# Adjacency of a graph layer in one-chunk steps, with one-hots shared by POOL and VectorE and filler products on TensorE

## The reference

```
h = layernorm(x);  q, k, v = linear(h) each
scores = sum(q[dst] * k[src]) / 16 + edge_weight * we + be
attn = exp(scores - segment_max[dst]) / segment_sum(exp)
out = segment_sum(v[src] * attn, dst)
x1 = layernorm(h + out + h @ ws + bs)
x2 = layernorm(x1 + ffn(x1));   x = x + x2
x = x + relu(W2[e] @ relu(W1[e] @ layernorm(x)))    with e = argmax of the router
```

## Time and profile before

| | us |
|---|---|
| median of 3 runs | 1888.78 |
| lowest, highest | 1887.14, 1910.01 |
| span of the profiled execution | 1885.6 |
| TensorE busy in it | 1656.9 |
| VectorE busy | 1193.9 |
| ScalarE busy | 965.5 |
| POOL busy | 300.8 |

### The profile page before, as it was taken

One profiled execution on the slowest core, in us unless ns is written; L12 is line 12 of the kernel. 1 busy time (PEld: TensorE's weight loads), 2 busy tenths in 40 slices (PEclk: granted clock), 3 DMA queues, 4 the chain that ended last, 5 costly groups with the idle time before them and its releaser, 6 DMA issues.

```text
span 1885.6 us, 41069 instructions
## 1 busy us (share of the span) xinstructions
PE 1656.9 (88%) x11015; PEld 1378.6 (73%) x11015; DVE 1193.9 (63%) x3327; ACT 965.5 (51%) x2962; POOL 300.8 (16%) x397
## 2 busy tenths in 40 slices
PE   2898999999799999999899999999999789419960
PEld 1796888888688888887688888888888779315640
DVE  3927898988688889898555555555555578701111
ACT  1566888888588888887233333333333345103210
POOL 0022000000000000000111111111110067375435
PEclk9999999999899999999999999999999889656555
DMA  6054333333433333334822222222210100047634
GB/s 159 28 129 115 104 105 104 106 103 105 140 104 104 106 105 103 104 105 112 164 76 77 76 76 76 76 78 75 76 75 37 53 17 0 6 117 214 181 113 121
DMA packets 226999, 180.40 MB, mean 96 GB/s; under 512 B 41884, under 2 KB 218038, under 8 KB 223544
## 3 DMA queue, kind: packets, MB, share of 16 engines
q1 hardware_dynamic: 189327, 112.46, 21.6%
q0 software_dynamic: 21408, 61.20, 9.7%
q10 hardware_dynamic: 16224, 6.27, 1.5%
HBM read 84.94 MB, written 99.11 MB: 98 GB/s over the span
## 4 chain that ended last, share of the span: by engine, by line
PE 78%; DVE 6%; DMA 5%; POOL 4%; issue 3%; SPq 2%; ACT 1%; POOLq 0%; DVEq 0%; ACTq 0%
PE bank L1371 29%; PE bank L1404 15%; PE bank L1392 11%; PE bank L1356 9%; PE bank L1411 3%; PE bank L1486 3%; PE bank L1493 2%; PE bank L1478 2%; PE bank L1444 2%; PE bank L1436 2%; POOL arena L691 2%; POOL xs_dram L669 2%; SPq L458 1%; DMA V<-in_x 1%; DMA arena<-in_x 1%
## 5 line engine op out<-in xcount | busy, mean ns | idle before, releaser
L784 ACT ACTIVATE arena<-bank,tables 128x128 f32<-128x128 f32 x2048 | 585.2, 369 | 144.5 <-PE bank L1356 144.4
L1371 PE MATMUL bank<-arena 128*125 128x128 f32 x4096 | 585.9, 286 | 11.8 <-DVE arena L1055 11.8
L1371 PEld LDWEIGHTS bank<-arena 128*125 128x125 f32 x4096 | 488.4, 188 | 65.1 <-DVE arena L1055 11.9
L1055 DVE TENSOR_TENSOR arena<-iota_row,tables 128x250 f32<-128x250 f32 x1024 | 421.1, 412 | 0.1
L1081 DVE SCALAR_TENSOR_TENSOR arena<-arena,tables,bank 125x128 f32<-125x128 f32 x1023 | 351.9, 344 | 86.5 <-PE bank L1371 37.1
L1404 PE MATMUL bank<-V,arena 125*125 125x256 f32 x1250 | 296.4, 382 | 5.6 <-ACT arena L810 5.6
L810 ACT COPY arena<-bank 125x500 f32<-125x500 f32 (+1 forms) x175 | 90.8, 533 | 379.5 <-PE bank L1411 379.5
L1404 PEld LDWEIGHTS bank<-V,arena 125*125 125x125 f32 x1250 | 223.3, 188 | 38.0 <-ACT arena L810 10.3
L1122 DVE CUSTOM_DVE_ANT_0 arena<-arena 125x3200 f32<-125x3200 f32 x25 | 87.3, 3493 | 222.2 <-ACT arena L793 222.2
L622 POOL COPY gidx<-arow 125x1 uint32 (+1 forms) x25 | 36.4, 1455 | 1182.2 <-DVE wk_sb L1122 856.7
L1356 PE MATMUL bank<-dist_rhs,arena 5*128 5x128 bf16 x2048 | 201.6, 218 | 4.2 <-DVE tables L1039 3.4
(11 more groups left out here) (219 smaller groups left out, 1665.5 us busy)
## 6 DMA issues: line engine op xcount, KB each, us to landing
adj<-arena SPq DMA_DIRECT2D x512, 125.0 KB
xs_dram<-zeros SPq DMA_DIRECT2D x64, 112.0 KB, 3.2
V<-xs_dram SPq DMA_DIRECT2D x56, 128.0 KB, 2.3
ys_dram<-arena SPq DMA_DIRECT2D x56, 128.0 KB, 1.9
w_dram<-in_L_ffn_W SPq DMA_DIRECT2D x2, 2048.0 KB
V<-in_x SPq DMA_DIRECT2D x5, 625.0 KB
q_dram<-arena ACTq DMA_DIRECT2D x25, 125.0 KB, 2.3
wq_sb<-q_dram SPq DMA_DIRECT2D x25, 125.0 KB, 7.8
```

The lines of the kernel that those rows point to most:

```text
L784: ins = nc.scalar.activation(Ys[:, q, k, :], bank[2 + s][:, k * LO:(k + 1) * LO], ACT.Relu, scale=nval_tab[:, bass.ds(i, 1)])
L1055: ins = V_.tensor_tensor(Xs[:, s, cols, :], iota_row[:, 0:TILE].unsqueeze(1).to_broadcast([P, SUB, TILE]), code_tab[:, bass.ds(g * GC + k ...
L1371: ins = mm(o, Xs[:, j % STAGES, k, :], Ys[:, j % STAGES, k, :], start=(k % SUB == 0), stop=(k % SUB == SUB - 1))
```

## The change

A step has one chunk. The blocks of sources are 128 wide and lie side by side (`HI` = 25 blocks of `LO` = 128), so keys and scores have 25 x 125 = 3125 columns, padded to 3136 = 7 x 448, in place of 25 x 128. There are 1406 steps, 704 groups, 44 turns. A group has two distance products, two activations, two one-hots, two products, two sums. The two distance products read from partitions 0 to 4 and 32 to 36 and write to different PSUM banks. One-hots: of eight groups the second, fifth and eighth (`OWN`) are VectorE's, in one instruction of 128x250 behind the group's second sum; the other five are POOL's, two instructions of 128x125 each, with codes copied to `held` first. TensorE does two bf16 products of 256 columns, whose result is not used, ahead of the products of every group, and waits before them for the sums of four groups earlier, a wait that it has twice. A put is two transfers, of 112 and of 13 partitions. The products in `keep_clock` are fillers too. The first gathers of adj come behind POOL's last one-hot. Edge table gathers: 11 in place of 16. Step counts run over 784 columns in 11 blocks.

```diff
-SUB = 2
+SUB = 1
-LO = 128
-ROW = NT * LO
+HI, LO = 25, 128
+ROW = HI * LO
+MW = WIN * HI
+PARTS = 2
+KB = 448
+NCOL = 7 * KB
-SCH = [(c, min(512, ROW - c)) for c in range(0, ROW, 512)]
+SCH = [(c, KB) for c in range(0, NCOL, KB)]
...
+        OWN = (1, 4, 7)
...
-                sp.dma_start(adj_v[:, bass.ds(g * GROUP, GROUP), :],
-                             stage[0:TILE, j % STAGES, :, :]).then_inc(stored[j % STAGES], 16)
+                for rows_ in (slice(0, EVEN), slice(EVEN, MW)):
+                    sp.dma_start(adj_v[rows_, bass.ds(g * GROUP, GROUP), :],
+                                 stage[rows_, j % STAGES, :, :]).then_inc(stored[j % STAGES], 16)
...
+            def one_hots(g, j, i):
+                h = j // LOADG
+                if j % LOADG == 0:
+                    pool.wait_ge(codes_held, 2 * i + h + 1)
+                if j % LOADG == 2 and not (isinstance(i, int) and i == TURNS - 1 and h):
+                    wait_from(pool, x_ready, pool_groups(j - 2, i))
+                    hold_codes(2 * i + h + 1, 1 - h)
+                if j % LOADG in OWN:
+                    return
+                wait_from(pool, prod_done, g - STAGES + 1)
+                pool.sem_inc(pool_mark, 1)
+                for k in range(GC):
+                    c = j % LOADG * GC + k
+                    ins = nc.gpsimd.tensor_scalar(Xs[:, j % STAGES, k, :], iota_row[:, 0:MW], held[:, h, c:c + 1], None,
+                                                  ALU.is_equal)
+                ins.then_inc(x_ready, 1)
...
+            def one_hots(g, q):
+                V_.tensor_tensor(Xs[:, q, :, :], iota_row[:, 0:MW].unsqueeze(1).to_broadcast([P, GC, MW]),
+                                 code_tab[:, bass.ds(g * GC, GC)].unsqueeze(2).to_broadcast([P, GC, MW]),
+                                 ALU.is_equal).then_inc(own_x_ready, 1)
...
                     ins.then_inc(sum_ord if k < GROUP - 1 else sums_ready, 1)
-                    if not (isinstance(i, int) and i == TURNS - 1 and j > BODY - STAGES):
-                        one_hot(g + STAGES - 1, (q - 1) % STAGES, k)
+                last = isinstance(i, int) and i == TURNS - 1 and j > BODY - STAGES
+                if (j + STAGES - 1) % LOADG in OWN and not last:
+                    one_hots(g + STAGES - 1, (q - 1) % STAGES)
...
+                    rows_ = slice(k * STRIP, k * STRIP + DIST)
+                    ins = mm(dist_bank(s, k)[:, 0:LO], dist_rows[rows_, j // LOADG, c:c + CHUNK], dist_rhs[rows_, :],
                              start=True, stop=True)
...
-                pe.wait_ge(x_ready, g + 1)
+                if j % LOADG in OWN:
+                    pe.wait_ge(own_x_ready, groups_before(j, i, True) + 1)
+                else:
+                    pe.wait_ge(x_ready, pool_groups(j, i) + 1)
+                wait_from(pe, sums_ready, g - STAGES + 1)
+                wait_from(pe, sums_ready, g - STAGES + 1)
+                idle_cols = product_bank(j)[:, GROUP * LO:2 * GROUP * LO]
+                for _ in range(2):
+                    mm(idle_cols, ones[:, :].bitcast(BF16)[:, 0:P], ones[:, :].bitcast(BF16), start=True, stop=True)
                 for k in range(GC):
```

More of the change, by code:

```diff
@@ L176, in gnn_moe @@
         assert SBLK * SUB * TABW <= edges_only
-        cmp_o = view(4 * P)
-        s_row, o_row, iota_c = view(4 * P), view(4 * P), view(4 * P)
-        cmp_s, s_row, o_row, iota_c = (v[:, 0:NS] for v in (cmp_o, s_row, o_row, iota_c))
+        cmp_o = view(NS)
+        s_row, o_row, iota_c = view(NS), view(NS), view(NS)
+        cmp_s = cmp_o
         diag_flat = view(SBLK * P)
@@ L329, in gnn_moe @@
         x_t = x.rearrange("(t p) d -> p t d", p=TILE)
[L330 removed]
+        xs_v, ys_v = (v.ap()[0:MT * P, :].rearrange("(j p) d -> p j d", p=P) for v in (xs_dram, ys_dram))
         out_t = out.rearrange("(t p) d -> p t d", p=TILE)
@@ L424, in product_bank, with groups_before, pool_groups, dist_bank @@
             return bank[j % 2 + 4 * (j % STAGES // 2)]
+        OWN = (1, 4, 7)
+        def groups_before(j, i, own):
+            mine = [r for r in range(LOADG) if (r in OWN) == own]
+            return i * (BODY // LOADG) * len(mine) + j // LOADG * len(mine) + sum(r < j % LOADG for r in mine)
+        def pool_groups(j, i):
+            return groups_before(j, i, False)
+        def dist_bank(s, k):
+            return bank[2 + s + 4 * k]
         def j_bank(first, s):
@@ L599, in _ @@
                         gath[:, b, u, :], None, edge_tab.ap()[:, :],
-                        bass.IndirectOffsetOnAxis(ap=cidx[:, u, b:b + 1], axis=0)).then_inc(gath_in[b], 16)
-            nc.gpsimd.memset(dist_rows[0:2, :, :], 1.0).then_inc(ones_set, 1)
+                        bass.IndirectOffsetOnAxis(ap=cidx[:, u, b:b + 1], axis=0)).then_inc(gath_in[b // 2], 16)
+            pool.wait_ge(ws_set, KH + 1)
+            for k in range(GC):
+                if k:
+                    pool.wait_ge(ones_set, k)
+                nc.gpsimd.memset(dist_rows[k * STRIP:k * STRIP + 2, :, :], 1.0).then_inc(ones_set, 1)
             pool.wait_ge(arow_set, 1)
@@ L609, in _, with hold_codes @@
             pool.wait_ge(q_stored[1], 16 * (NT // 2))
+            pool.wait_ge(ones_set, GC)
+            pool.wait_ge(tab_set, SBLK)
+            pool.wait_ge(terms_stored, 16 * SUB * SBLK)
+            def hold_codes(n, h):
+                nc.gpsimd.tensor_copy(held[:, h, :], code_tab[:, bass.ds(n * HELD, HELD)]).then_inc(codes_held, 1)
+            hold_codes(0, 0)
+            def one_hots(g, j, i):
[9 more added lines that the diff above has]
+                pool.sem_inc(pool_mark, 1)
+                for k in range(GC):
+                    c = j % LOADG * GC + k
+                    ins = nc.gpsimd.tensor_scalar(Xs[:, j % STAGES, k, :], iota_row[:, 0:MW], held[:, h, c:c + 1], None,
+                                                  ALU.is_equal)
+                ins.then_inc(x_ready, 1)
+            turns(pool, one_hots)
             last_group = (2 * TILE // WIN + NS - 2) // GROUP
@@ L799, in key_parts @@
                 c, n = SCH[b]
-                j = slice(c // LO, (c + n) // LO)
-                nc.scalar.copy(k_hi[:, :, j, :], kT[:, :, j, :]).then_inc(k_hi_set, 1)
+                nc.scalar.copy(k_hi[:, :, c:c + n], kT[:, :, c:c + n]).then_inc(k_hi_set, 1)
             def weights(t, s, t_next, u):
@@ L1332, in _, with keep_clock @@
             ins.then_inc(rows_bc, 1)
+            def keep_clock(n):
+                for _ in range(n):
+                    mm(bank[1][:, 0:FF], ones[:, :], wf1_sb[:, 0, :], start=True, stop=True)
+            pe.wait_ge(params_in, 16 * len(params))
+            pe.wait_ge(s_copied, 2)
+            keep_clock(2)
             for b in range(SBLK):
```

143 lines of the change are left out of this document (74 added, 69 removed).

## The result

The changed kernel takes 2089.24 us (median of 4 runs, 2081.95 to 2094.61) against 1893.63 us for the kernel before in the same session: a ratio of 1.099, 95% interval 1.093 to 1.105. It is slower, as forecast, but by more than twice the forecast +90 us, and outside the range of 1895 to 2065. The profiled execution took 2090.43 us with a span of 2088.2, so 202.6 more than the 1885.6 of before.

A forecast was written before the change was run, and what follows sets the result against it. VectorE's dependent sums were taken to bound the changed adjacency stage at 1.15 us a group. Stage +82, start of attention +10, attention -10 and before the stage +8 gave +90 on the median 1888.8, so 1978 us; range 1895 to 2065.

The forecast's parts named there:

- SP's sum: Adjacency stage: SP's two stores with register work 0.75 us a group, plus 0.1 for zeroes and row loads, under 1.15.
- The others per group: Adjacency stage: ScalarE and POOL wait, SP almost fills; all stay under VectorE's 1.15 us a group.
- The rival that did come: Adjacency stage: POOL's or SP's rate, or the stores' landing, bounds at 1.25 to 1.35 us a group; chance 0.12.
- VectorE's group: Adjacency stage: two dependent sums, 0.51 and 0.63 us, plus own one-hots make 1.15 us a group, the bound.
- put at 1.06 us: Adjacency stage, TensorE per group: distances 0.21, switch 0.19, products 0.44, fillers 0.22 us; bounds 0.9 to 1.3.
- The first rival: Adjacency stage: waits between sums are hidden, TensorE stays the bound at 1.0 to 1.06 us a group, say 1893 us; chance 0.2.
- the third rival: Adjacency stage: TensorE's granted clock falls from 2.4 to 1.2 GHz, 1.7 us a group, some 2370 us; chance 0.06.
- the 0.73 that I took as dearest: Adjacency stage: POOL's price per one-hot from its dearest near row, an addition; two make 1.46 us, so POOL keeps up.
- the doubling that the prediction weighed: Adjacency stage: VectorE's own one-hots may double beside POOL; 0.02 us a group taken, bounds 0 and 0.15.
- Before the stage: Ahead of the first distances: longer step counts +15, fewer gathers -6, shorter memset -1, so +8 us; bounds 0 and +16.
- Start of attention: Last sum to first mask: the later first gather of adj lands 13 to 18 us after the last sum, +10 us.
- Attention: Scores in 7 x 448 columns save 0.4 us on each of 25 tiles, -10 us; bounds -12 and 0.

The follow-up runs named there:

- the paired run: Changed kernel with eight buffers of sums instead of four and both stores issued once for two groups: 1963.07 us, ratio 1.037.

## Why the prediction was wrong

**The step that failed is SP's sum, in "The others per group":** "with register work, 0.75 us a group, plus zeroes and two row loads each eight groups, 0.1: under 1.15". It put SP at 0.85 us a group, behind VectorE's 1.15. SP takes 1.08 us for the stores (0.31 to 0.34 each and 0.17 to 0.27 of register work and gaps behind each, where I had taken 0.264 and 0.11) and 0.2 for the rest, so 1.29, and is the bound. I had priced an issue by its own row and not by the distance to the next. 704 groups at 1.29 instead of 1.15 are 99 us, the whole miss in the stage. The rival that did come, POOL's or SP's rate at 1.25 to 1.35 us with 2049 to 2120 us, stood in the prediction with 12 chances in 100, and its "against" was empty: before, no wait for a store could show, as SP then had 383 us to spare. That the kernel is slower was not luck: with half of SP's issues taken away it is what the prediction described, bound by VectorE's chain, and at 1963 us near the 1978 forecast.

**VectorE's group** was predicted at 1.15 us. Behind SP it was not the bound; with SP free it was 1.112, its two dependent sums 0.50 and 0.59 apart where I had 0.51 and 0.63. This mechanism was right, but not the bound. Half sums that alternate run 0.22 us apart for 0.28 us each, whole ones that wait for each other 0.50 for 0.35, some 0.12 of it register work behind the wait. The Trainium skill ("VectorE: DVE Perf Modes", section The DRAIN you can't avoid) says of its own test that a semaphore after each op cost nothing extra; in this loop the wait for the op right in front did cost.

**TensorE**, put at 1.06 us, needed 0.92 and was not the bound in any run of the changed kernel with fillers. The first rival is refuted by the paired run, where the group took 1.11. The clock fell only to 0.95, and to 0.50 without fillers, so the third rival's condition was real, and the fillers are what keeps it away here. Its price was too high: at the lower level, though without fillers, a group took 1.35 us and not 1.7.

**POOL** needed 0.60 us a one-hot, below the 0.73 that I took as dearest. The own one-hots went from 0.41 to 0.454 us at the median, 0.62 at most: +0.04, not the doubling that the prediction weighed. The doubling was the price that L1190 had beside a POOL addition; the Trainium skill ("GPSIMD Engine Reference", section Key points) names the contention and no price.

**Before the stage**: +17 for +8, just past its upper bound of +16, and not all of it is the change's. The last gather of the edge table is issued at 155.22 us instead of 144.42, 10.8 later, where the sum made it 9. In the chain of the profile after stand two waits of ScalarE for something that the profile does not name, and the clock-keeping products (L1399), which were put into waiting time (start us, us, what):

```profile
147.44 4.40 another core or an unknown queue
...
152.99 5.30 another core or an unknown queue
...
163.66 1.72 PE bank L1399 x4
...
170.78 3.43 PE bank L1399 x8
174.21 0.24 PE bank L1429 x4
```

The kernel before has no such wait, and its first distances start at 157 us. But in the run of it with two stores, whose edit lies behind this stretch, the same wait is in the chain, and they start at 170.6:

```profile
132.03 16.61 another core or an unknown queue
```

In three profiles of versions of the changed kernel without such a wait (half sums, and blocks of 512 with and without halved sums) they start at 166.2, 166.9 and 169.2 us, so 9 to 12 later than before. The forecast of +8 was about right for these. What ScalarE waits for, and why only in some profiles, stays open.

**Start of attention**: +8 for +10, by the mechanism forecast, a gather of 19.88 us on the chain from 1081.68.

**Attention**: +8.5 for -10. The products do come every 0.20 us, as worked out, but TensorE then runs into VectorE. Two rows of TensorE's timeline in one tile of the profile after, the idle time and its releaser in brackets:

```profile
1309.42 0.36 PE L1471 MATMUL bank<-k_hi,q_lo 128*125 128x448 f32 x1
1310.32 0.47 PE L1471 MATMUL bank<-k_hi,q_hi 128*125 128x448 f32 x1 [0.53 <-DVE wk_sb L1174]
```

The fifth block of a tile needs the first block's bank, and VectorE's guard (L1174) hasn't read it yet. 0.90 us pass instead of 0.20. The 0.4 that a tile saves on columns is paid with 0.7. I had written "TensorE has no slack there" and not asked who would be late next. The run with blocks of 512 columns bears it out: -0.3 us a tile, and TensorE's wait for this guard, 23 times between 1120 and 1655 us in the profile after, is there once.

**Behind the last mask** the 11 us are no effect of the change: in the experiments the same stretch lasted between 414 and 451 us from one profiled execution to another, on either kernel. In two runs of the kernel before with other stores it took 420 us at a granted clock of 0.75 and 451 at 0.66.

## What to carry to other kernels

A queue that only issues DMAs has no busy column: before an edit adds an issue to it, measure the distance from one issue to the next in its chain, register work included, and compare its wait time before with what is added. When a saving is taken at its full size, name the engine that will be late next; here a second issue in each group, fewer columns per product, and a later gather each met one. Two dependent operations on an engine cost their latency; cutting each into two independent halves that alternate gave 60 us back, though the instructions were twice as many.

## What the runs showed of the hardware

- Stores of 125 partitions moved at most 125 KB in 1.24 us, with four buffers or eight, and landed in 3.4 to 4.6 us wherever one stood on the chain with four; split into 112 and 13 the store landed in some 1.5 us. With eight buffers SP's issue of such a store took 832 ns at the median in place of 264.
- SP's issue took 264 ns for 125 partitions, 322 for 112, 312 for 13, but 610 to 620 for 64, and 450 or 320 for 48, by its place.
- Leaving the fillers out of TensorE's work made the kernel 54 us slower (2143.58 against 2089.24, the stage 44 us longer): the granted clock stood at 0.50 instead of 0.95.
- A VectorE sum of 64 columns took 0.280 us and one of 128 took 0.348; alternating, the halves started 0.22 us apart.
